# One-hots of a token routing as 16-bit numbers, with the pair's index innermost

## The reference

```python
x = x + 0.5 * ffn(layernorm(x), ...)
x = x + attn(layernorm(x), ...)
x = x + 0.5 * ffn(layernorm(x), ...)

def ffn(x, router_weight, w_in, w_out, bias):          # 8 experts, top 2, hidden 512
    logits = x @ router_weight.T
    top_vals, top_idx = top_k(logits, 2)
    gates = softmax(top_vals)
    for each expert e:
        a, b = split(x @ w_in[e].T)
        acc += gate[:, e] * (silu(a) * b @ w_out[e].T)
    return acc + bias
```

## Time and profile before

| | |
|---|---|
| time, median of three runs | 437.04 us (435.76 to 438.95) |
| profiled execution, its own time | 440.74 us |
| its span | 438.6 us |
| mean granted PE clock in it | 0.973 |

### The profile page before, as it was taken

The page is one execution under the profiler, slowest core; times in us unless marked ns, Lnnn a source line. Parts: engine busy times, 40 slices in busy tenths (PEclk is TensorE's granted clock), DMA queues, the critical chain, the costliest instruction groups (busy, mean ns, idle before and its releaser), DMA issues.

```text
span 438.6 us, 10176 instructions
## 1 busy us (share of the span) xinstructions
PE 408.5 (93%) x2911; PEld 333.9 (76%) x2912; DVE 300.8 (69%) x613; ACT 257.1 (59%) x638; POOL 247.7 (56%) x307
## 2 busy tenths in 40 slices
PE   7768999999999889799999999888799999999996
PEld 4536888888888867588887888764488888888884
DVE  6767996865556697777677676966365575556566
ACT  2706885555655455788787787822155655655552
POOL 5136445866467349657777577210365586754850
PEclk9679999999999999989999999996999999999999
DMA  8929931111211630000000000007551212112136
GB/s 278 371 68 347 389 100 59 47 51 60 59 48 36 190 109 1 1 1 2 4 1 0 0 0 0 1 1 252 153 184 49 62 37 72 60 48 52 44 103 208
DMA packets 25738, 38.90 MB, mean 89 GB/s; under 512 B 3056, under 2 KB 20720, under 8 KB 25712
## 3 DMA queue, kind: packets, MB, share of 16 engines
q1 hardware_dynamic: 19088, 24.41, 16.3%
q0 software_dynamic: 4544, 12.07, 9.4%
q10 hardware_dynamic: 2080, 2.10, 1.4%
HBM read 29.37 MB, written 9.19 MB: 88 GB/s over the span
## 4 chain that ended last, share of the span: by engine, by line
PE 65%; DVE 12%; DMA 10%; issue 5%; ACT 3%; POOL 2%; SPq 1%; DVEq 0%; ACTq 0%; POOLq 0%
PE bank L1301 24%; PE bank L1323 12%; PE bank L1459 7%; PE bank L1470 4%; PE bank L1311 3%; DMA xn_scratch<-arena 3%; PE bank L1224 3%; DMA w_out<-y_scratch 3%; PE bank L1426 2%; PE bank L1277 2%; PE bank L1506 2%; DMA arena<-xn_scratch,gather_row 2%; DVE w_lo L876 1%; DMA y_scratch<-arena,scatter_row 1%; PE bank L1460 1%
## 5 line engine op out<-in xcount | busy, mean ns | idle before, releaser
L509 POOL DMA_INDIRECT arena<-xn_scratch,gather_row x46 | 50.8, 1105 | 72.7 <-PE bank L1277 42.1
L515 POOL DMA_INDIRECT y_scratch<-arena,scatter_row x42 | 60.2, 1434 | 34.3 <-ACT arena L681 31.2
L1301 PE MATMUL bank<-w_hi,xT_hi 128*128 x184 | 62.6, 421 | 1.2 <-ACT xT_hi L640 1.2
L990 DVE TENSOR_TENSOR wo_lo<-w_out,wo_hi 128x1024 fp32r<-128x1024 f32 x46 | 60.8, 1321 | 4.1 <-PE bank L1323 1.9
L995 DVE TENSOR_TENSOR gT_lo<-bank,gT_hi 128x512 fp32r<-128x512 f32 x46 | 31.7, 689 | 39.3 <-ACT gT_hi L655 39.2
L1301 PE MATMUL bank<-w_hi,xT_lo 128*128 x184 | 58.1, 397 | 0.0
L1301 PE MATMUL bank<-w_lo,xT_hi 128*128 x184 | 57.8, 395 | 0.0
L593 POOL TENSOR_TENSOR k_head<-k_hi,head_mask 128x256 fp32r<-128x256 f32 x64 | 38.7, 625 | 29.1 <-PE bank L1460 22.2
L648 ACT ACTIVATE arena<-bank 128x512 f32<-128x512 f32 x46 | 27.5, 598 | 45.7 <-PE bank L1301 45.7
L670 ACT ACTIVATE wo_hi<-w_out 128x1024 fp32r x46 | 48.8, 1060 | 6.0 <-issue 4.1
L979 DVE TENSOR_TENSOR xT_lo<-bank,xT_hi 128x256 fp32r<-128x256 f32 x46 | 19.5, 424 | 39.0 <-ACT xT_hi L640 38.9
(11 more groups left out here) (180 smaller groups left out, 968.8 us busy)
## 6 DMA issues: line engine op xcount, KB each, us to landing
w_raw<-in_win_t SPq DMA_DIRECT2D x8, 1024.0 KB, 9.7
w_out<-in_wout_t SPq DMA_DIRECT2D x16, 512.0 KB, 8.0
w_out<-y_scratch SPq DMA_DIRECT2D x16, 256.0 KB, 4.9
xn_scratch<-arena ACTq DMA_DIRECT2D x2, 1024.0 KB, 8.7
x<-in_x SPq DMA_DIRECT2D x4, 256.0 KB, 3.6
out<-x SPq DMA_DIRECT2D x4, 256.0 KB, 2.1
arena<-xn_scratch,gather_row POOLq DMA_INDIRECT x46, 3.5
y_scratch<-arena,scatter_row POOLq DMA_INDIRECT x46, 3.0
```

The costliest lines, as they stand in the source:

```text
L509: pool.indirect_dma_start(out=xb[j % 2][:, :], out_offset=None, in_=xn_dram, in_offset=bass.IndirectOffsetOnAxis(ap=gather_row[:, j:j + 1] ...
L515: pool.indirect_dma_start(out=y_dram, in_=y[j % 2][:, :], in_offset=None, out_offset=bass.IndirectOffsetOnAxis(ap=scatter_row[:, j:j + 1], ...
L990: dve.tensor_tensor(wo_lo[:, :, :], w_out[:, bass.ds(e, 1), :, :].rearrange("p o c d -> p (o c) d"), wo_hi[u][:, :, :].bitcast(F32), ALU.s ...
L1301: last = pe.matmul(bank[2 * half + u][:, :], tok[u][:, k, :], wts[:, bass.ds(e, 1), k, half * H:(half + 1) * H], start=(part == 0 and k == ...
```

## The change

The one-hots are laid out with the pair's index innermost: `row_hot` [128 rows, 16 pairs], `blk_hot` [23 blocks, 16 pairs], both 16-bit. What they are compared with is no longer a constant row that is broadcast, but a table of the same shape, `row_nos` and `blk_nos`, 16-bit, in free room of the arena. POOL writes the two tables with iotas in `number_hots()`, before `ffn(0)` and again before the last inverse root ahead of `ffn(1)`, there after a wait for the last transpose of the attention's probabilities (their room is the same). DVE copies `row_i` to 16 bits (`row_h`), writes the block numbers to `block_h`, waits for `nos_ready`, and compares 16-bit numbers; `pair_id` is 16-bit too, and the product with it is made in place. The pair matmuls read both operands with a step of 16 elements. The numbers of fillers stay as they are.

```diff
-        row_hot, at_hot = view(arena, at, [PAIRS, P], F16)
-        blk_hot, at_hot = view(arena, at_hot, [PAIRS, BLOCKS])
-        blk_pair, at_hot = view(arena, at_hot, [PAIRS, BLOCKS], F16)
+        row_hot, at_hot = view(arena, at, [P, PAIRS], F16)
+        blk_hot, at_hot = view(arena, at_hot, [BLOCKS, PAIRS], F16)
+        row_nos, at_hot = view(arena, at_hot, [P, PAIRS], F16)
+        blk_nos, at_hot = view(arena, at_hot, [BLOCKS, PAIRS], F16)
...
-        pair_id = sb("pair_id", [P, PAIRS])
+        pair_id = sb("pair_id", [P, PAIRS], F16)
...
+        block_h = sb("block_h", [P, PAIRS], F16)
+        row_h = sb("row_h", [P, PAIRS], F16)
...
+            def number_hots():
+
+                pool.iota(row_nos[:, :, :], [[1, P], [0, PAIRS]], base=0, channel_multiplier=0,
+                          allow_small_or_imprecise_dtypes=True)
+                pool.iota(blk_nos[:, :, :], [[1, BLOCKS], [0, PAIRS]], base=0, channel_multiplier=0,
+                          allow_small_or_imprecise_dtypes=True).then_inc(nos_ready, 1)
...
+            number_hots()
             ffn(0)
...
             inverse_root(2, 0, TPAIRS - 1)
+
+            pool.wait_ge(probsT_done, BATCH * HEADS)
+            number_hots()
             inverse_root(2, TPAIRS - 1)
             ffn(1)
...
-                def one_hot_rows(q):
-                    shape = [P, q.stop - q.start, P]
-                    return mark(dve.tensor_tensor(row_hot[:, q, :], bc(row_i[:, q], 2, shape), bc(col[:, :], 1, shape),
-                                                  ALU.is_equal))
-
-
                 dve.wait_ge(route_step, row_at)
-                one_hot_rows(slice(0, PAIRS // 2))
+                row_at = mark(dve.tensor_copy(row_h[:, :], row_i[:, :]))
+                dve.wait_ge(nos_ready, f + 1)
+
+                def one_hot_rows(rows):
+                    return mark(dve.tensor_tensor(row_hot[:, rows, :], bc(row_h[:, :], 1, [P, rows.stop - rows.start, PAIRS]),
+                                                  row_nos[:, rows, :], ALU.is_equal))
+
+
+                dve.wait_ge(route_step, row_at)
+                one_hot_rows(slice(0, P // 2))
...
-                one_hot_rows(slice(PAIRS // 2, PAIRS))
+                one_hot_rows(slice(P // 2, P))
                 dve.wait_ge(route_step, block_at)
-                block_at = mark(dve.tensor_tensor(block_of[:, :], block_of[:, :], blk_i[:, :], ALU.add))
+                block_at = mark(dve.tensor_tensor(block_h[:, :], block_of[:, :], blk_i[:, :], ALU.add))
...
-                then(dve.tensor_tensor(blk_hot[:, :, :], bc(block_of[:, :], 2, [P, PAIRS, BLOCKS]),
-                                       bc(block_no[:, :], 1, [P, PAIRS, BLOCKS]), ALU.is_equal))
-                dve.tensor_tensor(blk_pair[:, :, :], blk_hot[:, :, :], bc(pair_id[:, :], 2, [P, PAIRS, BLOCKS]), ALU.mult)\
+                then(dve.tensor_tensor(blk_hot[:, :, :], bc(block_h[:, :], 1, [P, BLOCKS, PAIRS]), blk_nos[:, :, :],
+                                       ALU.is_equal))
+                dve.tensor_tensor(blk_hot[:, :, :], blk_hot[:, :, :], bc(pair_id[:, :], 1, [P, BLOCKS, PAIRS]), ALU.mult)\
                     .then_inc(hot_ready, 1)
...
-                    last = pe.matmul(bank[7][:, 0:BLOCKS], row_hot[:, q, :], blk_pair[:, q, :], start=(q == 0),
+                    last = pe.matmul(bank[7][:, 0:BLOCKS], row_hot[:, :, q], blk_hot[:, :, q], start=(q == 0),
```

More of the change, by code:

```diff
@@ L165, in build @@
         xnT, at = view(arena, at, [DK, T])
-        row_hot, at_hot = view(arena, at, [PAIRS, P], F16)
-        blk_hot, at_hot = view(arena, at_hot, [PAIRS, BLOCKS])
-        blk_pair, at_hot = view(arena, at_hot, [PAIRS, BLOCKS], F16)
+        row_hot, at_hot = view(arena, at, [P, PAIRS], F16)
+        blk_hot, at_hot = view(arena, at_hot, [BLOCKS, PAIRS], F16)
+        row_nos, at_hot = view(arena, at_hot, [P, PAIRS], F16)
+        blk_nos, at_hot = view(arena, at_hot, [BLOCKS, PAIRS], F16)
+        assert at_hot <= arena.shape[1]
         xb, y = [None] * 2, [None] * 2
@@ L277, in build @@
         hot_ready = sem("hot_ready")
+        nos_ready = sem("nos_ready")
         pairs_done = sem("pairs_done")
```

## The result

Before and after were timed again side by side: the median is 443.61 us after (442.19 to 445.08, six runs) and 438.50 before (435.76 to 439.03, six runs). That is 5.1 us slower, and 6.3 us over the forecast of 437.3. The measured ratio is 1.0124, interval 1.0087 to 1.0161.

The account below looks back on a forecast made before the run. PE was taken as the bound (busy 93%), with its filler queue last at the second routing. Terms of 0, −0.1 + 0.4 and 0 gave +0.3 us on the median 437.04: 437.3 us, range 434.8 to 439.5.

Parts of the forecast that it names:

- Contention: DVE's scalings of two tiles beside POOL's second tables: no delay, 0 taken, upper bound 1.9 us.
- scalings well over 0.4 us near 286: Sign listed as proving the prediction wrong: DVE's scalings while POOL makes the second tables.
- An iota reads nothing: Reason given for 0 contention, beside a row where scalings next to an iota ran undisturbed, two in 0.73 us.
- rival 4: After first routing: earlier fillers shift PE's low clock in the projections, −1.65 us (435.7) or +1.3 (438.6); chance 0.15, both directions.
- The first routing is hidden by the store: First routing: the plan is ready earlier, but POOL's first gather still waits for the token store; 0 gained.
- The stride: Second routing's 16 pair matmuls, operands read 16 elements apart: +25 ns each, +0.4 us; bounds nothing to +1.2 us.
- The pure sum: First routing 0, second routing −0.1 + 0.4, contention 0: +0.3 us.
- Rival 1: Second routing: fillers at full clock end early, DVE is last, full 1.2 us gain counts, less 0.4: 436.2 us; chance 0.2.
- Rival 2: Second routing's pair matmuls: strided weights at the 32-bit price, 107 ns each, +1.2 us less 0.1: 438.1 us; chance 0.15.
- Rival 3: Second routing's one-hots stay at 1.05 ns an element, ready at 308.1: +0.2 + 0.4, 437.6 us; chance 0.05.

Follow-up runs that it names:

- run 2: Kernel before, with only the second routing's tables written by POOL iotas at the change's place and never read: 1.0083, 3.6 us.
- run 1: Changed kernel with the second pair of tables written only after DVE's last scaling: 1.0035 to the kernel before.
- run 6: Changed kernel with the row table written by 16 iotas of 128 elements in place of one of 2048, same place: 1.0037 to the kernel before.
- run 4: As run 2, with memsets of the same 2048 and 368 elements in place of the iotas: 1.0034 to the kernel before.
- run 9: Changed kernel with 12 fillers ahead of line 1253's transposes, where PE idles while DVE's scaling is held: 1.0071 to the kernel before.
- run 3: As run 1, with 13 fillers in place of 18 ahead of the second routing's pair matmuls: 0.9995 to the kernel before.
- Runs 11 and 12: 14 fillers in place of 6 behind the first routing's plan: on run 3, 0.9977; on the kernel before with nothing else, 0.9972.
- run 5: Kernel before with only the pair's index innermost; 32-bit comparisons with broadcast constants, no tables: 1.0023.
- run 7: Changed kernel with the tables written after the first pair of tiles is scaled (18 scaled tiles): 1.0047 to the kernel before.

## Why the prediction was wrong

*The step that failed is "Contention".* It took 0 with an upper bound of 1.9 us; the runs show a hold of 2.4 us on the chain. The tables alone on the kernel before cost 3.6 us (run 2), and writing them later takes most of the loss away (run 1). The place was right, POOL's slow rows were in view, and scalings well over 0.4 us near 286 were on the list of what would show the prediction wrong. Three things were wrong.

- The row chosen for the value was the wrong size. In the earlier trace rows the iota beside the scalings is of 23 elements. In run 6 short iotas beside the same two scalings cost them nothing (0.74 us). Even that row had the sign in it: the iota took 0.31 us where one of that size took 0.16, so one engine did wait for the other. The question was how long a single POOL instruction is, and the prediction had worked that out (0.14 us + 2048 × 0.8 ns = 1.8, measured 2.48).
- The upper bound used the slowest scaling seen, 1.32 us, held by an add of 1.27 us. The bound should have been the length of the new instructions, which the prediction itself put at 2.2 us for both tables and at 5.5 us at the most.
- "An iota reads nothing" was no reason: a memset of the same size holds DVE too (run 4).

*What comes on top of the hold was left out.* The prediction priced a hold at its own length. At about equal clock that fits the traces: 2.5 us in the stretch. But the loss is 5.1 us, and the stride accounts for 0.4 of it. PE's idle time became 3.33 us in place of 0.94, and 2.56 us of fillers at the low clock stood ahead of the context's transposes. With PE kept busy through most of that time the ratio goes from 1.0124 to 1.0071 (run 9), which is some 2.3 us. The two intervals just overlap, so this size is rough. That the idle time makes the low clock more likely is argued from this and from the traces under run 9, not shown: the same low clock came without any hold in four of ten. A low clock was weighed for the first routing (rival 4) and not here.

*The base moved.* Six runs of before have their median at 438.5, three had it at 437.0; 1.5 of the 6.3 us by which the forecast missed are this. The chance given to a loss of more than 1% was 0.03.

*What held.* The one-hots took 0.69 and 0.34 us, and ended 1.2 us earlier counted from the ranks (4.28 us after `placed` begins, against 5.45). The fillers ended last, so that none of this came through. The first routing is hidden by the store. The stride costs 0.98 − 0.54 = 0.44 us on the chain, predicted 0.4. POOL had the time for both tables, 3.1 us in place of 2.2, and its roots were not late. The pure sum, without contention, was +0.3 us; run 1, which has everything of the change but the hold, stands at +1.5 us by the ratio, and run 3, with five fillers fewer, at 0.9995.

*Rivals.* Rival 1 was seen in run 1's profile. Rival 2, the stride at the 32-bit price of 107 ns, did not come: 1.20 us for 16 is 75 ns each at most. Rival 3, one-hots as slow as before, fell (0.69 us). Rival 4's mechanism is there: in the changed kernel the projections took 4.16 us against 4.40, with 1.1 us more for the transposes and fillers ahead of them (0.69 + 1.71 against 0.44 + 0.86), and the projections end at 34.74 against 34.54, 0.2 us later. Runs 11 and 12 suggest that some 1.2 us can be had there.

*What stays open.* With the tables late the kernel is still at 1.0035; the stride accounts for 0.4 to 0.6 us of these 1.5, and run 5, the stride alone, could not be told from 1. How much of the rest is real isn't settled. Nor is the reason why PE's clock falls in one execution and not in another of the same instructions.

## What to carry to other kernels

Before a long instruction is put on POOL "where it is idle", look at what DVE does on the chain in the same microseconds: a one-source DVE operation in SBUF may wait for the whole of it, and for the next one too (run 4). Iotas of 128 elements did little harm (run 6); moved behind DVE's scalings, the long ones made no DVE operation beside them longer (run 1). When a delay on the chain is priced, look at PE's clock behind it as well: it moved the same stretch by up to 2.4 us with nothing held. And before an operation is made faster, read which instruction ends last at the meeting point: here nearly all of the 1.2 us gained on DVE stood behind a fixed count of fillers.

## What the runs showed of the hardware that was not expected

- DVE's one-source scaling (128x256, 32-bit, from SBUF to SBUF) ended only behind POOL's instruction: 2.55 us beside an iota of 2.48, and 2.21 us beside memsets of 1.80 and 0.40 in a row; 0.41 beside iotas of 128 elements. DVE's two-input operations in SBUF beside the long iota were not held (run 7, 0.76 us for two), nor its reductions from PSUM (1.28 us for two).
- Beside a POOL instruction that reads SBUF, DVE's two-input operations are not safe either. In the kernel before, DVE's subtraction of 1024 elements at line 990 took 3.99 us beside the add from 76.23 to 80.86, where the median of 46 is 1.23:

```profile
77.95 3.99 DVE L990 TENSOR_TENSOR wo_lo<-w_out,wo_hi 128x1024 fp32r<-128x1024 f32 x1
```

- The Trainium skill (GPSIMD Engine Reference, "8. Key points") says that GpSimd shares its interfaces to SBUF with the vector engine, in contention with instructions in a two-port mode or with two inputs in SBUF. Which mode the scalings run in no run shows; that they are held agrees if it is such a mode. For two inputs the runs show both: contention beside POOL's add (3.99 us), none beside its iota (run 7).
- The Trainium skill (VectorE: DVE Perf Modes, "What auto-detection actually checks") has two elements a cycle for a two-tensor operation on 16-bit operands. The trace agrees with the half: 1024 elements in 0.69 us against 1.22, with one input read again and again by a step of 0 in the outer dimension. With the same layout and 32-bit inputs it stayed at 1.22 (run 5).
- 16-bit weight loads with a step of 32 bytes took 143 to 182 ns against 94 to 100 packed, and 16 pairs of load and matmul 0.4 to 0.6 us more. The Trainium skill (SBUF — State Buffer, "Door 1: The DMA port swizzle") has a penalty for each step to a new line. The runs agree; the layout costs some 30 to 40 ns for a matmul of 128 weight columns and 23 moving ones. Both operands were strided, so that the share of each is not separated.
